# First block of the last feed-forward layer worked inside the tail of the last self-attention, in a perceiver kernel on one core

## What is computed

```python
x = x + _L1_attn_ref(_layernorm(x, axis=-1), Wqkv, bqkv, W1p, W2p, plucker_scale, Wout, bout)
x = x + _L1_ffn_ref(_layernorm(x, axis=-1), w1_w, w1_s, w2_w, w2_s, h1_w, h1_s, h2_w, h2_s, w3_w, w3_s)

def _L1_attn_ref(x, ...):            # 16 heads, causal, 32 positions
    lines_h = plucker_lines(x @ W1p, x @ W2p)          # six numbers a head, scaled to length 1
    logits = q @ k.T * dh ** -0.5 + (lines_h @ Jlines.T) * plucker_scale
    return (softmax(causal(logits)) @ v) @ Wout + bout

def _L1_ffn_ref(x, ...):             # 256 -> 1024 -> 1024 -> 1024 -> 256, all fp32
    h = silu(_tlin(x, w1_w, w1_s)) * _tlin(x, w2_w, w2_s)
    h = gelu(_tlin(h, h1_w, h1_s))
    h = gelu(_tlin(h, h2_w, h2_s))
    return _tlin(h, w3_w, w3_s)
```

## Time and profile before

| | |
|---|---|
| time, three runs | 1577.23, 1579.0, 1583.18 us, median 1579.0 |
| the profiled execution | 1576.78 us, its span 1575.0 us |
| busy share of the span | TensorE 93%, DVE 57%, ACT 45%, POOL 32% |
| mean granted TensorE clock | 0.985 |
| last self-attention | about 850 to 1002 us |
| last feed-forward layer | from there to the end |

### The profile page before, as it was taken

One profiled execution on the slowest core, in us unless ns is written; L12 is line 12 of the kernel. 1 busy time (PEld: TensorE's weight loads), 2 busy tenths in 40 slices (PEclk: granted clock), 3 DMA queues, 4 the chain that ended last, 5 costly groups with the idle time before them and its releaser, 6 DMA issues.

```text
span 1575.0 us, 33033 instructions
## 1 busy us (share of the span) xinstructions
PE 1459.0 (93%) x12564; PEld 1127.3 (72%) x12564; DVE 895.5 (57%) x1889; ACT 713.0 (45%) x1764; POOL 503.2 (32%) x697
## 2 busy tenths in 40 slices
PE   6999997997999999999997888699999999999998
PEld 5877775445777777777775666368858886886887
DVE  5988996479546666666665888443234224323332
ACT  6887775398635555555553656222212212211221
POOL 2445551001026966965656777100000000000000
PEclk9999998999999999999998999899999999999999
DMA  8000000006132162145210000113413430431230
GB/s 299 21 7 2 1 0 21 0 0 194 48 120 69 53 241 72 54 160 220 60 40 1 2 0 0 47 47 140 154 47 105 163 120 30 158 140 60 94 140 14
DMA packets 60510, 123.99 MB, mean 79 GB/s; under 512 B 5008, under 2 KB 15760, under 8 KB 57872
## 3 DMA queue, kind: packets, MB, share of 16 engines
q1 hardware_dynamic: 60432, 122.94, 22.4%
HBM read 108.24 MB, written 14.68 MB: 78 GB/s over the span
## 4 chain that ended last, share of the span: by engine, by line
PE 69%; DVE 15%; POOL 8%; issue 4%; ACT 2%; DVEq 0%; DMA 0%; SPq 0%; POOLq 0%; ACTq 0%
PE ps L944 23%; PE ps L537 15%; PE ps L543 5%; PE ps L741 5%; PE ps L735 4%; PE ps L995 4%; PE ps L761 3%; PE ps L713 3%; POOL R L1968 2%; DVE R L1367 2%; DVE R L1664 2%; POOL R L1950 2%; PE ps L772 2%; DVE amax L1538 2%; POOL R L1942 1%
## 5 line engine op out<-in xcount | busy, mean ns | idle before, releaser
L944 PE MATMUL ps<-R 128*128 128x256 f32 x1792 | 388.6, 379 | 3.5 <-DVE R L1805 3.5
L944 PEld LDWEIGHTS ps<-R 128*128 128x128 f32 x1792 | 340.0, 190 | 52.3 <-issue 6.5
L537 PE MATMUL ps<-R 128*128 128x128 f32 (+1 forms) x1344 | 306.8, 388 | 6.0 <-DVE R L1534 4.3
L537 PEld LDWEIGHTS ps<-R 128*128 128x128 f32 x1344 | 190.2, 194 | 118.7 <-issue 109.5
L1239 ACT ACTIVATE R<-ps,c_nmx 128x257 f32<-128x257 f32 x256 | 118.1, 474 | 126.4 <-DVE c_nmx L1688 126.4
L1950 POOL TENSOR_TENSOR R<-R,c_inv 128x1024 f32<-128x1024 f32 x64 | 121.0, 1891 | 130.6 <-DVE c_inv L1699 130.6
L1664 DVE COPY R<-ps 128x512 f32<-128x512 f32 x128 | 88.2, 689 | 81.9 <-PE ps L761 80.6
L741 PE MATMUL ps<-x_wv,R 128*128 128x256 f32 x512 | 121.1, 379 | 0.0
L2041 POOL TENSOR_SCALAR g_ve<-g_mv 128x4 f32<-128x4 f32 x4 | 0.9, 236 | 345.5 <-DVE g_mv L1767 345.5
L741 PEld LDWEIGHTS ps<-x_wv,R 128*128 128x128 f32 x512 | 92.5, 190 | 10.1
L735 PE MATMUL ps<-R,x_wk 128*128 128x256 f32 x384 | 95.7, 391 | 0.0
(11 more groups left out here) (211 smaller groups left out, 2518.9 us busy)
## 6 DMA issues: line engine op xcount, KB each, us to landing
R<-quadrant_sums SPq DMA_DIRECT2D x32, 1024.0 KB, 6.8
R<-in_f_hq SPq DMA_DIRECT2D x32, 768.0 KB, 4.6
R<-in_ctxT SPq DMA_DIRECT2D x64, 257.0 KB, 2.7
R<-in_f_hq SPq DMA_DIRECT2D x8, 1024.0 KB, 8.3
quadrant_sums<-R SPq DMA_DIRECT2D x8, 1024.0 KB, 8.3
R<-in_ctxT SPq DMA_DIRECT2D x16, 256.0 KB, 3.9
k_ahead<-R SPq DMA_DIRECT2D x16, 256.0 KB, 3.9
R<-k_ahead SPq DMA_DIRECT2D x16, 256.0 KB, 3.1
```

Of the source, the lines that this page charges most:

```text
L537: r = mm(dst, w[:, ki, fo * P:(fo + 1) * P], src[:, ki, :], start=(ki == 0), stop=(ki == KI - 1))
L944: r = mm(ps[:, 4 * (g % 2) + bk, half * HALF:(half + 1) * HALF], f_wr[g % 3][:, w, ki * P:(ki + 1) * P], src[:, k, ki, :], start=(ki == 0) ...
```

## The change

Block 0's first steps move up into the last round and the tail of the attention.

- `run_lanes` takes a table of things to do after a given slot of the last round ("last") or of the tail ("tail"). Where the table is given, the last round is written out instead of being the loop's last pass.
- DVE: two statistics after slot 4 of the last round and two after slot 11, the aggregations after slot 14, the normalisation after slot 27.
- POOL: `g_rsqrt(0)` after slot 18 of the last round.
- TensorE: `g_turn(0)` after slot 3 of the tail, then pairs 0, 1 and 2 half by half after slots 6, 10, 13, 15, 17 and 19. Half pair i = 0 of pair o waits for lane o's last addition, since it writes lane o's banks.
- ACT: `g_turned(0)` after slot 6 of the tail. SiLU still comes after all lanes' last additions.
- Memory: `f_xn` goes to the place of `f_c11` and `f_u4` behind w3, `f_xnT` and `f_silu` into lane 0's part of R; the others follow. Block 0 is turned into banks 0 and 1.

```diff
-        f_xn, f_xnT = view(a[2], TPB, D), view(a[3], KI, BLK)
-        f_silu = view(a[4], 2, BLK)
+        f_xn, f_xnT = view(f_w3_end, TPB, D), view(a[0], KI, BLK)
+        f_silu = view(a[1], 2, BLK)
...
+        turned_bank = lambda b, ki: 5 + 2 * ki if b else ki
...
-        def run_lanes(eng, slots, stages):
+        def run_lanes(eng, slots, stages, between=None):
...
+                    if between and (name, slot) in between:
+                        between[name, slot]()
...
-                with eng.Fori(1, NT) as i:
+                with eng.Fori(1, NT - 1 if between else NT) as i:
                     a_round(i, steps, i - 1, steps)
+                if between:
+                    a_round(NT - 1, steps, NT - 2, steps, "last")
                 behind = steps
-            a_round(NT, (), NT - 1, behind)
+            a_round(NT, (), NT - 1, behind, "tail")
...
+            def g_pair(b, o, i):
+
+                if i == 0:
+                    if o == 0:
+                        pe.wait_ge(g_xTc, 2 * b + 2)
+                    if b == 0 and o < NL:
+                        pe.wait_ge(s["x_updated"], tile(3 * NT - 1, o))
...
+                      {("tail", 3): lambda: g_turn(0),
+                       ("tail", 6): lambda: g_pair(0, 0, 0), ("tail", 10): lambda: g_pair(0, 0, 1),
+                       ("tail", 13): lambda: g_pair(0, 1, 0), ("tail", 15): lambda: g_pair(0, 1, 1),
+                       ("tail", 17): lambda: g_pair(0, 2, 0), ("tail", 19): lambda: g_pair(0, 2, 1)})
             for b in range(NB):
-                g_first(b)
+                for o in range(0 if b else 3, NF1):
+                    for i in range(2):
+                        g_pair(b, o, i)
...
+                (18, a_keys), (23, a_exp), (24, a_pT), (27, a_oT))])], {("tail", 6): lambda: g_turned(0)})
...
+            def two_stats(t):
+                dve.wait_ge(s["x_updated"], tile(2 * NT, NL - 1))
+                g_stat(0, t)
+                g_stat(0, t + 1)
...
+                      {("last", 4): lambda: two_stats(0), ("last", 11): lambda: two_stats(2),
+                       ("last", 14): lambda: g_aggregate(0), ("last", 27): lambda: g_normalise(0)})
...
+                      {("last", 18): lambda: g_rsqrt(0)})
...
-            with pool.Fori(0, NB) as b:
+            with pool.Fori(1, NB) as b:
                 g_rsqrt(b)
```

More of the change, by code:

```diff
@@ L226, in perceiver @@
         c_quad = [view(R1 + i * QUAD, QUAD) for i in range(6)]
-        a = put(0, [7 * 4 * HALF] * 2 + [1024, 1024, 1024, 512, 512, 512, 256, 768, 7 * BLK])
+        a = put(0, [KI * BLK, 2 * BLK] + [7 * 4 * HALF] * 2 + [512, 512, 512, 256, 768, 512, 7 * BLK])
         assert a[-1] + 7 * BLK <= R1
-        f_a, f_b = view(a[0], 7, 4, HALF), view(a[1], 7, 4, HALF)
+        f_a, f_b = view(a[2], 7, 4, HALF), view(a[3], 7, 4, HALF)
         B11, B21, B22, T1, T2, T4, B12 = range(7)
@@ L232, in perceiver @@
         A11, A12, A22, S1, S2, S3, S4 = range(7)
-        f_xn, f_xnT = view(a[2], TPB, D), view(a[3], KI, BLK)
-        f_silu = view(a[4], 2, BLK)
[L235 to L239, removed]
+        f_xn, f_xnT = view(f_w3_end, TPB, D), view(a[0], KI, BLK)
+        f_silu = view(a[1], 2, BLK)
+        f_y = view(a[4], 2, D)
+        f_p1, f_u2 = view(a[5], 2, HALF), view(a[6], 2, HALF)
+        f_u3 = view(a[7], HALF)
+        f_c22, f_c21, f_c12 = (view(a[8] + i * HALF, HALF) for i in range(3))
+        f_c11, f_u4 = (view(a[9] + i * HALF, HALF) for i in range(2))
+        turned_bank = lambda b, ki: 5 + 2 * ki if b else ki
         f_wr = [view(at, 7, BLK) for at in f_wr + [a[10]]]
@@ L348, in perceiver, with a_round @@
         SLOTS0, SLOTS1 = 20, 28
-        def run_lanes(eng, slots, stages):
+        def run_lanes(eng, slots, stages, between=None):
             lag = slots // NL
-            def a_round(i, steps, i_behind, steps_behind):
+            def a_round(i, steps, i_behind, steps_behind, name=None):
                 for slot in range(slots):
@@ L902, in p_turn_last @@
                     pe.wait_ge(c_x, T)
-                if not (l < 2 and isinstance(n, int)):
+                if not (l < 2 and isinstance(n, int) and n == NORM[A1]):
                     p_turn(kind, l, n)
             def p_project_last(kind, l, n):
-                if not (l < 2 and isinstance(n, int)):
+                if not (l < 2 and isinstance(n, int) and n == BASE[A1]):
                     p_project(kind, l, n)
[L911 to L920, removed]
             def g_turn(b):
@@ L927, in g_turn @@
                     for t in range(TPB):
-                        r = tr(ps[:, 5 + 2 * ki, t * P:(t + 1) * P], f_xn[:, t, ki * P:(ki + 1) * P], ident[:])
+                        r = tr(ps[:, turned_bank(b, ki), t * P:(t + 1) * P], f_xn[:, t, ki * P:(ki + 1) * P], ident[:])
                     r.then_inc(g_xT, 1)
-            def g_first(b):
-                pe.wait_ge(g_xTc, 2 * b + 2)
-                for o in range(NF1):
+            def g_pair(b, o, i):
[4 more added lines that the diff above has]
+                        pe.wait_ge(s["x_updated"], tile(3 * NT - 1, o))
                     if o >= 4:
@@ L938, in g_first @@
                     project(ps[:, 2 * (o % 4), :], f_w1, f_xnT, o)
+                else:
                     project(ps[:, 2 * (o % 4) + 1, :], f_w2, f_xnT, o).then_inc(g_ab, 1)
@@ L996, in g_last @@
                     r.then_inc(g_w3, 1)
-            g_turn(0)
+            pe.wait_ge(in_w["ffn"], 16 * 3)
+            run_lanes(pe, SLOTS1, [
+                (lambda: None, [(0, lambda l, i: p_turn_last(A1, l, i + NORM[A1])),
+                                (4, lambda l, i: p_project_last(A1, l, i + BASE[A1]))]
+                 + attention(A1, "a1", [(12, p_slots), (15, p_scores), (20, p_turn_probs),
+                                        (22, p_values), (24, p_turn_out), (26, p_out)])[1])],
+                      {("tail", 3): lambda: g_turn(0),
+                       ("tail", 6): lambda: g_pair(0, 0, 0), ("tail", 10): lambda: g_pair(0, 0, 1),
+                       ("tail", 13): lambda: g_pair(0, 1, 0), ("tail", 15): lambda: g_pair(0, 1, 1),
+                       ("tail", 17): lambda: g_pair(0, 2, 0), ("tail", 19): lambda: g_pair(0, 2, 1)})
             for b in range(NB):
-                g_first(b)
+                for o in range(0 if b else 3, NF1):
+                    for i in range(2):
+                        g_pair(b, o, i)
                 for h in range(2):
@@ L1021, in a_scale @@
                 if kind == A1:
-                    if isinstance(n, int) and l < 2:
+                    if isinstance(n, int) and n == NORM[A1] and l < 2:
                         act.wait_ge(s["nmr_ready"], last_norm(l))
@@ L1287, in of_last @@
                 return at_tile
[L1289 to L1295, removed]
             def g_turned(b):
@@ L1299, in g_turned @@
                     act.wait_ge(g_xT, 1 + 2 * b + ki + 1)
-                    af(f_xnT[:, ki, :], ps[:, 5 + 2 * ki, :], ACT.Copy).then_inc(g_xTc, 1)
+                    af(f_xnT[:, ki, :], ps[:, turned_bank(b, ki), :], ACT.Copy).then_inc(g_xTc, 1)
             def g_first(b):
@@ L1325, in g_close @@
                 af(dst[:, B12, f, :], f_c12, ACT.Gelu, scale=upper).then_inc(g_c, 1)
-            g_turned(0)
+            run_lanes(act, SLOTS1, [(lambda: None, [(at, of_last(step)) for at, step in (
+                (1, a_scale), (5, a_xnT), (9, a_lines), (12, a_values), (16, a_spread_values),
+                (18, a_keys), (23, a_exp), (24, a_pT), (27, a_oT))])], {("tail", 6): lambda: g_turned(0)})
+            for l in range(NL):
+                act.wait_ge(s["x_updated"], tile(3 * NT - 1, l))
             for b in range(NB):
@@ L1750, in of_last, with g_stat, g_aggregate @@
                 return at_tile
[L1752 to L1756, removed]
             xb = x[:, :, :].rearrange("p (b t) d -> p b t d", t=TPB)
-            def g_norm(b):
-                for t in range(TPB):
-                    v.bn_stats(g_stats[:, t, :], xb[:, b, t, :]).then_inc(s["stats_ready"], 1)
+            def g_stat(b, t):
+                v.bn_stats(g_stats[:, t, :], xb[:, b, t, :]).then_inc(s["stats_ready"], 1)
+            def g_aggregate(b):
                 dve.wait_ge(s["stats_ready"], NORMS + TPB * b + TPB)
@@ L1767, in g_norm, with g_normalise @@
                     v.bn_aggr(g_mv[:, t, :], g_stats[:, t, :]).then_inc(s["mv_ready"], 1)
+            def g_normalise(b):
                 dve.wait_ge(s["rstd_ready"], NORMS + b + 1)
@@ L1774, in g_norm @@
                 r.then_inc(g_xn, 1)
+            def g_norm(b):
+                for t in range(TPB):
+                    g_stat(b, t)
+                g_aggregate(b)
+                g_normalise(b)
+            def two_stats(t):
+                dve.wait_ge(s["x_updated"], tile(2 * NT, NL - 1))
+                g_stat(0, t)
+                g_stat(0, t + 1)
             def two(ap):
@@ L1837, in g_last @@
```

(15 more changed lines are left out.)

## The result

The changed kernel takes 1565.76 us, the median of 4 runs (1565.20 to 1569.54); the kernel before, with one more run of it, 1578.12 (1577.15 to 1583.18). The ratio is 0.992, its 95% interval 0.9893 to 0.9947. The prediction was 1568, in a range of 1562 to 1574, with a gain of 10.8 us; measured are 12.4 between the medians and 11.5 between the two profiled spans (1575.0 and 1563.5).

The account below looks back on a forecast made before the run. Bound: a serial chain from attention's end to the first layer, with TensorE mostly idle for 8.50 us. The span shrinks from 39.6 to 24.2 us, 15.4 gained; less 3.7 and 0.9, 10.8: 1579.0 becomes 1568, range 1562 to 1574.

Parts of the forecast that it names:

- The new wait: Last round: POOL's norm steps wait for DVE's aggregation before lane 1, so TensorE's L587 of lane 1 comes 3.7 us late.
- Nothing of it comes back: Lanes after the stall: a closed chain of L587, L1367 and scores, so none of the 3.7 us is recovered.
- Clock: After the stall in mid-attention, one 3.4 us stretch at the 1.2 GHz level, costing 0.9 us, between 0 and 1.7.
- DVE's part: DVE under attention: statistics hidden, aggregation costs nothing, normalisation before lane 3's lsq puts 1.4 us on the end chain.
- The tail: Up to the last out-projection, with products in the gaps: 4.4 us later, at 1004.5, the 3.7 left out.
- After it: Last out-projection to the first layer's end: out-projection 0.9, half a pair 1.7, five pairs 17.2 us; clock stays up.
- The sum: Whole kernel: 15.4 us gained, 3.7 and 0.9 lost, so 10.8, giving 1568; a gain of 9 to 12 had 0.50.
- A side estimate: By the skill's figure, five half pairs before the last out-projection are worth 4.3 us, not 8.6; gain some 4 smaller.
- POOL's wait did cost: The rival on POOL's queue before lane 1 said its wait costs nothing: gain 15.4 us, 1563.6; chance 0.10.
- the products do fit: The rival in the tail said they don't: lane 3's chain lengthens 10.9 us, not 4.4; gain 4.3, 1574.7; chance 0.13.
- the slower case: Rival after the stall: TensorE stays at 1.2 GHz through the three lanes left; 16.4 us lost, 1595; chance 0.05.
- The clock falls in the tail too: Rival in the tail: two 3.4 us stretches at half speed cost 3.4 more; gain 7.4, 1571.6; chance 0.20.

Follow-up runs that it names:

- e1: Changed kernel with POOL's two norm steps after slot 25 of the last round instead of slot 18: 1562.29 us, ratio 0.9905 to the kernel before.
- e2: Changed kernel with DVE's aggregation after slot 12 of the last round instead of slot 14: 1562.80 us, ratio 0.9909 to the kernel before.
- e8: The changed kernel measured and profiled again, nothing altered: 1564.89 us, ratio 0.9922 to the kernel before.
- e3: Changed kernel without products in the tail, all eight pairs of block 0 behind the attention: 1575.14 us, ratio 0.9983 to the kernel before.
- e7: The same kernel as e1, run and profiled once more: one run, 1559.06 us.
- e6: On top of e1: half pairs one place up in the tail, aggregation after slot 12, normalisation split over slots 25 and 27: 1561.05 us.

## Why the prediction was right, step by step

- **The new wait.** Forecast 3.7 us at L592 of lane 1; measured 3.50 and 3.48. The links were each forecast within 0.3: POOL idle 4.4 (4.23), lane 1's first step 4.9 late (4.62), DVE idle 3.5 before its reduction (3.58). e1 removes it by moving POOL's two steps, e2 shortens it by the amount that POOL's wait gets shorter.
- **Nothing of it comes back.** From lane 0's scores to lane 1's it is 8.63 us before (967.23 to 975.86) and 12.93 after (966.59 to 979.52); from lane 1's to lane 2's it is 8.63 again (to 988.15). The 4.30 are 3.50 of stall and 0.80 of clock.
- **Clock.** Forecast one low stretch of 3.4 us costing 0.9, between 0 and 1.7. It came in all three profiles with this stall; it cost 0.80 in the changed kernel's, 0.5 in e8 (966.92 to 979.12 and on to 988.18 is 21.26, less 17.26 for two periods and 3.48 of stall) and 0.5 in e3 (968.85 to 990.13, 21.28, with 3.50 of stall). One in the tail cost 1.65 (e1 against e7). The 0.9 was the middle between two bounds, so that 0.80 came so close is in part luck.
- **DVE's part.** Statistics hidden: each pair stands before an addition (L1454 at 954.82 and 963.44) that no longer waits, and L1373 still has 0.40 idle before it, so nothing is late. Normalisation 1.4 on the end chain: from lane 0's scores to L592 of lane 3 it is 21.81 us before (to 989.04) and 27.45 after (to 994.04), 5.64 more, of which 4.30 are stall and clock and 1.34 are left. e6 takes half of it out and gains 0.67.
- **The tail.** Forecast 4.4 us later at the last out-projection, the stall and the clock left out. From lane 0's scores to it: 32.90 us before (967.23 to 1000.13), 41.73 after (966.59 to 1008.32), 8.83 more; less 4.30, that is 4.53.
- **After it.** Forecast 19.8 us to the end of the first layer (0.9 + 1.7 + 17.2); measured 19.74 (1008.32 to 1028.06), against 39.48 before. ACT's and DVE's part was hidden as said: the products L542 run from 1009.18 to 1028.06 without a wait.
- **The sum.** 10.8 forecast, 10.91 measured in the seam, with no term off by more than 0.2: the stall 0.20 too long, the clock 0.10 too dear, the tail 0.13 too short, the rest after it 0.06 too long, and the first layer's end taken from the end of its row (1039.76) where the next product starts at 1039.61. Some of these cancel. The 2.2 us between 1568 and 1565.8 are not in a step of the sum. I took the gain off a median of three runs, 1579.0, where a fourth run makes it 1578.1: 0.9. Of the other 1.3, 0.6 came before the seam in the profiles, and the rest is not located; it is less than the spread of the runs.
- **A side estimate.** The prediction's 4.3 us for the five half pairs, by the figure of the Trainium skill (TensorE: Matmul & The Clock Gate, "Back-to-back issue gap"), takes the 216 ns of a lone product for each record. Taken for each instruction of 512 columns, of which five half pairs have ten, it is an estimated 2.2 us. The sum did not use it, and the trace does not bear it out for these fp32 products: a half pair takes 1.72 (1006.60 to 1008.32).
- **The rivals.** POOL's wait did cost (e1); the products do fit (the tail's 4.53, and e3); the slower case didn't come: the low stretch ended after 3.4 us and the clock was 1.00 from 982 on. "The clock falls in the tail too" did not come in the changed kernel's two profiles; one such stretch came in e1's, at half the price of the two that the rival had.

## What to carry to other kernels

When a small chain is tucked into another engine's queue, follow its inputs, not its length: two POOL steps of 1.4 us in all cost 4.3 us because they stood ahead of a lane's work and waited for a DVE step that was still 4 us away. A step that waits belongs in the queue behind everything that could run meanwhile. Filling the gaps of a sparse tail with independent products was worth more here (8.3 us, 2.6 of them because the clock stayed up) than removing the serial start of the next layer (2.6 us with the stall, and an estimated 6.6 without it, e3's 4.0 of stall and low clock added back). Keep one piece of the products for behind the last step, to cover that step's own latency.

## What I had not expected of the hardware

The same program with the same wait (2.04 and 2.05 us before L592 of lane 3) had TensorE's mean clock at 0.60 over some 4 us behind it in one execution and at 1.00 in the next one. The seams of these two profiles differ by 1.65 us for that reason alone. And the seam began anywhere between 964.6 and 970.5 us in ten profiles, though what they do up to there is all but the same: a single total hides a step of 1 or 2 us, and the length of a stretch inside the trace shows it.
